# State space mixer on one Trainium2 core: decay rows of the third and fourth head pair loaded at other moments, into other stage buffers

## The reference, cut to what matters

```python
x_conv = jax.nn.silu(jnp.transpose(xc, (0, 2, 1)))
A = -jnp.exp(A_log)
dt = jax.nn.softplus(dt_proj + dt_bias)
dA = jnp.exp(A[None, None] * dt[..., None])
dB = B_proj * dt[..., None]
def step(h, inp):
    dA_t, dB_t, C_t, x_t = inp
    h = dA_t[..., None] * h + dB_t[..., None] * x_t[:, :, None, :]
    y_t = jnp.einsum('bns,bnsd->bnd', C_t, h)
    return (h, y_t)
...
y_heads = y_heads + D[None, None, :, None] * x_heads
y = y_heads.reshape(B, L, d) * jax.nn.silu(z)
return y @ W_out.T
```

## Time and profile before

| | |
|---|---|
| median of 3 runs | 976.01 us (974.56, 976.01, 976.02) |
| the profiled execution | 977.62 us |
| its span, first to last instruction | 975.8 us |
| mean granted TensorE clock | 0.882 |
| PE / DVE / ACT / POOL busy | 748.2 / 457.2 / 269.4 / 269.6 us |
| the pair loop in it, first L1214 to first L1262 | 537.9 to 620.7 us |

### The profile page before, as it was taken

How to read it: one execution, slowest core, us unless ns; L and a number is a source line. 1 busy time by engine, 2 the same in 40 slices (tenths; PEclk the granted TensorE clock), 3 DMA queues, 4 the chain that set the end, 5 groups by cost and what they waited for, 6 DMA issues and landing times. The chain is left out here.

```text
span 975.8 us, 19429 instructions
## 1 busy us (share of the span) xinstructions
PE 748.2 (77%) x6595; PEld 475.8 (49%) x6595; DVE 457.2 (47%) x1265; ACT 269.4 (28%) x532; POOL 269.6 (28%) x304
## 2 busy tenths in 40 slices
PE   5999999768664998897999569974466777776646
PEld 2455657236442454555544468752245554553315
DVE  3222334576664232324366378588684433432216
ACT  2122212454451121112236333032312222221150
POOL 1200000101340200000004265113147777776520
PEclk9999999778896999999799555778779999999878
DMA  9989990200287389992184550010158888889867
GB/s 356 394 325 384 416 402 13 86 1 2 55 318 292 135 348 350 410 402 106 33 177 90 132 133 4 3 43 1 30 168 246 254 259 251 250 249 306 257 222 308
DMA packets 70777, 200.36 MB, mean 205 GB/s; under 512 B 11912, under 2 KB 37744, under 8 KB 64944
## 3 DMA queue, kind: packets, MB, share of 16 engines
q1 hardware_dynamic: 60720, 176.29, 52.3%
q0 software_dynamic: 7680, 20.98, 6.7%
q10 hardware_dynamic: 2304, 2.10, 0.7%
HBM read 185.51 MB, written 13.83 MB: 204 GB/s over the span
## 5 line engine op out<-in xcount | busy, mean ns | idle before, releaser
L1896 PE MATMUL ps<-moe_wgu,moe_xgT 128*128 128x256 f32 (+1 forms) x320 | 90.5, 408 | 26.1 <-DMA moe_wgu_second<-moe_gate_up 15.9
L2014 POOL DMA_INDIRECT moe_xg<-xn_rows,moe_idx x80 | 78.5, 981 | 77.7 <-DVE moe_idx L1965 45.9
L2023 POOL DMA_INDIRECT y_rows<-moe_ysb,moe_row x80 | 79.3, 992 | 34.0 <-issue 17.1
L1884 PE MATMUL ps<-ident,moe_xg 128*128 128x128 f32 x160 | 36.3, 311 | 49.1 <-DMA moe_xg<-xn_rows,moe_idx 48.9
L1896 PEld LDWEIGHTS ps<-moe_wgu,moe_xgT 128*128 128x128 f32 (+1 forms) x320 | 53.8, 189 | 38.9 <-DVE moe_xgT L1970 17.2
L1369 POOL TENSOR_TENSOR ss_dec<-ss_dec,ss_cT 128x256 f32<-128x256 f32 x48 | 39.7, 862 | 101.0 <-ACT ss_dec L1334 51.0
L1998 ACT ACTIVATE moe_hs<-ps 128x128 f32<-128x128 f32 x80 | 22.2, 278 | 162.0 <-PE ps L1896 162.0
L1975 DVE TENSOR_TENSOR moe_hrow<-moe_hs,ps 128x128 f32<-128x128 f32 x80 | 22.9, 286 | 80.9 <-ACT moe_hs L1998 68.8
L1970 DVE COPY moe_xgT<-ps 128x256 f32<-128x256 f32 x80 | 33.9, 424 | 53.2 <-PE ps L1884 52.6
L1182 PE MATMUL ps<-xnT,w_win 128*128 128x512 f32 x128 | 58.8, 618 | 0.0
L1214 PE MATMUL ps<-ss_dec 64*64 64x32 f32 (+2 forms) x1792 | 46.1, 256 | 16.0 <-issue 14.5
(11 more groups left out here) (369 smaller groups left out, 1440.4 us busy)
## 6 DMA issues: line engine op xcount, KB each, us to landing
x0ctxT<-ctx_T SPq DMA_DIRECT2D x8, 3202.0 KB, 18.9
x1ctxT<-ctx_T SPq DMA_DIRECT2D x8, 3202.0 KB, 13.0
x0ctxN<-ctx SPq DMA_DIRECT2D x8, 3072.0 KB
x1ctxN<-ctx SPq DMA_DIRECT2D x8, 3072.0 KB
moe_wgu<-moe_gate_up SPq DMA_DIRECT2D x80, 256.0 KB, 3.5
moe_wdn<-L_ffn_We_down SPq DMA_DIRECT2D x80, 128.0 KB, 3.3
moe_yg<-y_rows SPq DMA_DIRECT2D x7, 1024.0 KB, 10.8
ss_dec<-seg_rows SPq DMA_DIRECT2D x8, 768.0 KB, 17.1
```

The costliest lines, as they stand in the source:

```text
L1884: mm = pe.transpose(ps[:, a2, h * P:(h + 1) * P], xg[:, a4, h * P:(h + 1) * P], ident[:])
L1896: mm = pe.matmul(ps[c * n_:(c + 1) * n_, 2 + a2, 0:2 * FE], xgT[:, a2, h, c * n_:(c + 1) * n_], src[:, a4, h, :, :].rearrange("p x f -> p ...
L2014: nc.gpsimd.indirect_dma_start(out=xg[:, a4, :], out_offset=None, in_=xn_rows, in_offset=bass.IndirectOffsetOnAxis(ap=idx[:, a4:a4 + 1], a ...
L2023: nc.gpsimd.indirect_dma_start(out=y_rows, out_offset=bass.IndirectOffsetOnAxis(ap=row[:, a4:a4 + 1], axis=0), in_=ysb[:, a4, :], in_offse ...
```

## The change

Pair 2's stages are now two pieces of `xi` behind the first 1024 columns (quarters 0 and 1), the piece of `xn` that held `segs` (quarter 2) and a piece of `win` (quarter 3). Quarter 2 is issued right after the loads of pairs 0 and 1, quarters 0 and 1 after the convolutions (`s_cv`), and only quarter 3 after the last projection. Pair 3 has stages in `win`, `xnT`, `xn` and `win`. Its quarters are issued one by one, when pair 2's same quarter has landed and 1, 3, 5 and 7 groups of products are done. Quarters 2 and 3 also wait for pair 2's exponentials, as they did. The number and the sizes of the transfers are the same: 16 of 384 KB.

```diff
-            stage = [x.rearrange("p (j l t) -> p j l t", j=2, l=LV) for x in
-                     (win[:].rearrange("p h e -> p (h e)")[:, 0:2 * SEG], win[:].rearrange("p h e -> p (h e)")[:, 2 * SEG:4 * SEG],
-                      xn_flat[:, 0:2 * SEG], xnT[:].rearrange("p h t -> p (h t)")[:, 0:2 * SEG])]
+            QUARTER = 2 * SEG
+            xi_flat, win_flat = xi[:].rearrange("p c b s -> p (c b s)"), win[:].rearrange("p h e -> p (h e)")
+            def quarters(*xs):
+                return [x.rearrange("p (j l t) -> p j l t", j=2, l=LV) for x in xs]
+            stage = {2: quarters(xi_flat[:, T:T + QUARTER], xi_flat[:, T + QUARTER:T + 2 * QUARTER], xn_flat[:, 0:QUARTER],
+                                 win_flat[:, 0:QUARTER]),
+                     3: quarters(win_flat[:, QUARTER:2 * QUARTER], xnT[:].rearrange("p h t -> p (h t)")[:, 0:QUARTER],
+                                 xn_flat[:, 0:QUARTER], win_flat[:, 0:QUARTER])}
...
+                    def load_quarter(c, q):
+                        for par in range(2):
+                            sp.dma_start(stage[c][q][64 * par:64 * par + 64].rearrange("p j l t -> p (j l t)"),
+                                         seg_rows[2 * c + par, 2 * q:2 * q + 2, :].rearrange("j x -> (j x)").partition_broadcast(64)
+                                         ).then_inc(s_lq[q], 16)
+                    load_quarter(2, 2)
+                    sp.wait_ge(s_cv, CI)
+                    load_quarter(2, 0)
+                    load_quarter(2, 1)
                     sp.wait_ge(s_pm, 4 * CI)
-                    for c in range(2, CI):
-                        for q in range(4):
-                            if c == 3:
-                                sp.wait_ge(s_e, exps[1] + q + 1)
-                            for par in range(2):
-                                sp.dma_start(stage[q][64 * par:64 * par + 64].rearrange("p j l t -> p (j l t)"),
-                                             seg_rows[2 * c + par, 2 * q:2 * q + 2, :].rearrange("j x -> (j x)").partition_broadcast(64)
-                                             ).then_inc(s_lq[q], 16)
+                    load_quarter(2, 3)
+                    for q in range(4):
+                        sp.wait_ge(s_lq[q], 32)
+                        sp.wait_ge(s_g, 2 * q + 1)
+                        if q >= 2:
+                            sp.wait_ge(s_e, exps[1] + q + 1)
+                        load_quarter(3, q)
...
-                            src = stage[q].rearrange("p j l t -> p (j l t)")
+                            src = stage[c][q].rearrange("p j l t -> p (j l t)")
```

## The result

The changed kernel takes 967.65 us (median of 4, 962.88 to 968.80) against 976.01. The ratio is 0.9899, with a 95% interval of 0.9856 to 0.9943, so 5.6 to 14.1 us less. Predicted were 969.1 and a range of 963.0 to 975.8.

The account below looks back on a forecast made before the run. The prediction took PE's fetch of instruction blocks, delayed by DMA traffic, to bound the pair loop. Gains of 6.1 - 0.9 + 1.7 = 6.9 us took the median from 976.0 to 969.1 us, range 963.0 to 975.8.

Parts of the forecast that it names:

- Blocks of instructions as the bound: Pair loop: PE gets some 256 instructions per block, 3.9 us per round trip in quiet, and runs dry when traffic delays one.
- Three quarters of pair 2 at no cost beside the projections: Before the loop: pair 2's quarters 0 to 2 load while PE issues few instructions; cost taken as zero.
- the slower rival: Before the loop: the new transfers share with pair 0's loads and delay the loop; 3.6 us slower, 979.6; chance 0.08.
- A: Loop's start: traffic of pair 2's quarter 3, data from 536.8 to 540.3; PE restarts at 543.3, not 545.2.
- Start of the loop and C: First groups: 6.1 us gained at the loop's start; C, pair 3's quarter 1 in a formerly quiet stretch, costs 0.9.
- B: Loop's start: traffic of pair 3's quarter 0 after the first group, data from 541.2 to 544.7; next block at 547.2.
- Bursts D and E: Later in the loop: pair 3's quarters 2 and 3 each meet an instruction packet, costing 2.5 us each; gain 1.7.
- DVE as the cap: Loop's quiet groups 8 to 12: DVE, busy 13.9 of 16.8 us, caps a full gain but not the predicted one.

Follow-up runs that it names:

- e2: Changed kernel with only pair 2 early; pair 3's quarters have their triggers of before. Ratio 0.9918 to the kernel before, loop 75.5 us.
- e3: Changed kernel with only pair 3 spread; all of pair 2 is loaded after the last projection. Ratio 0.9995 to the kernel before, loop 80.0 us.
- e5: Changed kernel plus 8 transfers of 256 KB into unread `win` after the last exponential. Ratio 0.9942 to the kernel before, loop 75.3 us.
- e4: Changed kernel without pair 3's transfers, its exponentials taken of pair 2's rows; two traces. Ratios 0.9858 and 0.9894 to the kernel before.
- e1: The changed kernel run again with no edit. Ratio 0.9921 to the kernel before, loop 72.5 us.
- e6: Changed kernel with pair 3's quarters 2 and 3 waiting for 7 and 8 groups, not 5 and 7; two traces. Ratios 0.9926 and 0.9931.
- e7: Changed kernel with pair 2's quarter 3 after two groups, pair 3's quarters after 3, 4, 5, 7; two traces. Ratios 0.9907 and 0.9913.
- e8: Kernel of e4 plus four 0.79 MB bursts after 5, 8, 11, 14 groups of products (first run) or gathers (second). Ratios 0.9919 and 0.9918.

## Why the prediction was right, and where it was off

**Blocks of instructions as the bound: right.** The pauses went where the traffic went (e2, e3) and came where it was put (e5). That the fetch is the bound in quiet too was right only in part: in the second trace of e4, PE goes from group 4 to 8 with no pause called issue.

**Three quarters of pair 2 at no cost beside the projections: right.** No stall is seen from them; the transposes, projections and clock stood as before. ACT's exponentials of pair 0 began at 507.63 in the trace after, 28.3 us before the loop, and at 509.66 before, 28.2 us before it. So the slower rival, transfers that share, is out. The traffic ran on from these loads without a break until 532.3, and A followed at 534.8.

**Start of the loop and C: right.** I had put 6.1 - 0.9 = 5.2 us. Measured to group 4: 5.0. The second long restart came 9.6 us after the loop's start and not 15.4, so 5.8 of the 6.1. C's pause of 1.35 us is 1.0 above the quiet ones. The packets of the first two blocks went out at the ends of A and B (538.0 and 542.75), as I had counted.

**Bursts D and E: the mis-sized term.** I put 2.5 us for each, 5.0 together, from counts in which the instruction packet falls 0.7 and 0.5 us into a burst. By the pauses there they cost 0.3 us in the first trace, 0.8 in e1 and 1.3 in e5, which has the same code up to its own transfers. The blocks there were not where I had put them. In the trace after, a packet goes out at 565.5 to 565.75, 0.5 us after SP's issue of D at 564.97 and some 1.0 us before its data, which begin at 566.5. The next ones go out at 569.5, in the lull between the data of D and E, and at 573.25, near the end of E. DMA queues in these two quarters of a microsecond:

```profile
q8 instruction: 1, 0.02, 26.8%
```

```profile
q1 hardware_dynamic: 14, 0.02, 46.1%
q8 instruction: 1, 0.02, 35.5%
```

In the first the instruction packet is the only thing that moves; in the second 14 of D's last packets are beside it, 0.02 MB where a quarter of a microsecond of full traffic has 0.06. Each burst lies nearly between two packets. Two things were wrong in my count. I had taken a packet to go out 1.9 us after the restart. In the trace of before one did (558.5 after 556.88), but those at 562.0, 565.5 and 583.75 followed their restarts by 0.9 to 1.4 us. With 1.2, my own count puts both packets at the very start of D and E and not 0.7 and 0.5 us into them. And I had carried the phase over from the trace of before, where the late blocks had set it. With these gone the phase was another, and e6 shows that it matters: 2 us later the same bursts give a 2.7 us pause. Gain from group 4 to 8: 6.8 us, predicted 1.7.

**DVE as the cap: right in kind, its cost left out.** I said that DVE caps a full gain but not this one. With D and E nearly free, it did: 1.1 us were given back in groups 8 to 15, where PE waits 1.06 and 2.03 us for `finish`. It is no chance: groups 8 to 15 took 30.6 to 31.3 us in the four traces whose stretch from group 4 to 8 was long (18.9 to 23.3: before, e2 and both of e6), and 32.3 to 33.4 in the seven where it was short (15.9 to 17.2: after, e1, e3, both of e4, both of e7).

Sum: 5.0 + 6.8 - 1.1 = 10.7 us of loop against 6.9 predicted, and 8.4 us between the medians. That the forecast time was right within 1.5 us is partly luck: the medians showed less than the loop gave, and this made up for most of the 3.8 us by which the loop's gain was put too small.

**What stays open.** Whether the loop's 10.7 us arrive in full in the time can't be told: the ratios of the two comparisons give 9.9 and 7.7 us, each with 3 to 4 us of uncertainty. The times of e1, e2 and e5 to e8 can't be told from each other either; only e3 stands apart. What is said of them rests on the traces, mostly on one each. Why the packets of a quiet loop are 3.3 to 4.0 us apart in one trace and another wasn't found. Nor was what holds an instruction packet back under traffic: in e3 two of them went out at 544.75 and 554.0, in the middle of transfers that ran from 538.5 to 557.1 us.

## What to carry to other kernels

Where an engine pauses for "issue" in the middle of code that has no waits, count its instructions and look at the instruction queues: a stage of many short matmuls can be bound by how fast its code arrives, and then a bulk transfer beside it can cost time though no one waits for its data. Move such transfers beside a stage with few long instructions. What is left goes in short pieces, with lulls between them; what a piece costs depends on its place within the round trip of the blocks (0.6 to 1.9 us in e8, and next to nothing for D and E in the changed kernel), and that place can't be carried over from a trace whose pauses are to go away.

## What the runs showed of the hardware

PE got its code in blocks of 256 instructions: 10 packets of 16 KB for the 2473 matmuls and loads at the end of the loop before the change. In quiet blocks the next packet went out 0.9 to 1.9 us after PE had begun on the block before, so only one was on its way at a time. Without traffic the packets were 3.3 to 4.0 us apart. Beside continuous traffic the restarts of PE were 8.1 and 8.9 us apart in the kernel before (223 and 217 GB/s), 9.2 in e3 and 7.0 in e2 (214 GB/s both), and beside a lone burst of 0.79 MB the packets came 0.6 to 1.9 us later than in quiet. At the granted clock of 0.50, 128 matmuls and their loads took about 3.2 us, so the loop was near the rate of the fetch even without traffic. The granted clock was 0.50 in the loop after 551 us with the pauses gone as well.
